# A fused scan and expert kernel: the turn loop written out, the expert tiles moved two units later, the scan output held twice

## What is computed

```python
xn = _layernorm(x)
# branch 1: scan over tokens sorted by cluster (16 states for each of 256 features)
buckets = argmax(scores);  xs = xn sorted by bucket (stable)
x_dbl = einsum('bdl,cd->bcl', u, x_proj_weight)      # dts, Bm, Cm (Cm += prompt)
delta = softplus(einsum('brl,dr->bdl', dts, dt_projs_weight) + bias)
h = exp(d_t * A) * h + (d_t * u_t) * b_t             # step over the tokens
y = einsum('bdn,bn->bd', h, c_t) + D * u             # then back in the order of x
# branch 2: top 2 of 8 experts, weighted by the softmax of their logits
h = silu(xt @ w1[e]) * (xt @ w3[e]);  y = h @ w2[e]
out = x + branch1(xn) + branch2(xn)
```

## Time and profile before

| | |
|---|---|
| median of 3 runs | 818.77 us (815.6 to 820.09) |
| the profiled execution | 817.38 us |
| its span, first to last instruction | 815.3 us |
| DVE busy | 682.9 us (84%) |
| PE busy | 663.9 us (81%) |
| POOL busy | 597.3 us (73%) |
| ACT busy | 431.0 us (53%) |

### The profile page before, as it was taken

How to read it: one execution, slowest core, us unless ns; L and a number is a source line. 1 busy time by engine, 2 the same in 40 slices (tenths; PEclk the granted TensorE clock), 3 DMA queues, 4 the chain that set the end, 5 groups by cost and what they waited for, 6 DMA issues and landing times. The chain is left out here.

```text
span 815.3 us, 15751 instructions
## 1 busy us (share of the span) xinstructions
PE 663.9 (81%) x4538; PEld 422.7 (52%) x4539; DVE 682.9 (84%) x882; ACT 431.0 (53%) x926; POOL 597.3 (73%) x372
## 2 busy tenths in 40 slices
PE   3734889788998798989998898999889798989870
PEld 2523745245655465556655565565556555655550
DVE  5769777579999999999999999999999999997110
ACT  1324656465655556656655575566557554653320
POOL 3728800038788898988989898888989898889532
PEclk9866955599999989999999998999999998999995
DMA  7972659979944754674575466547645654662322
GB/s 228 371 259 91 180 206 297 321 221 241 210 102 103 144 118 87 146 150 94 115 163 111 89 149 138 105 90 164 139 90 125 134 127 90 142 142 35 49 27 26
DMA packets 76845, 118.63 MB, mean 146 GB/s; under 512 B 22456, under 2 KB 56848, under 8 KB 74512
## 3 DMA queue, kind: packets, MB, share of 16 engines
q1 hardware_dynamic: 54656, 90.95, 41.2%
q0 software_dynamic: 19824, 27.16, 19.4%
q10 hardware_dynamic: 2336, 0.15, 0.2%
HBM read 82.87 MB, written 35.27 MB: 145 GB/s over the span
## 5 line engine op out<-in xcount | busy, mean ns | idle before, releaser
L534 POOL TENSOR_TENSOR ring<-ring,bc 128x1024 f32<-128x1024 f32 (+2 forms) x128 | 308.0, 2424 | 38.9 <-DVE state L1047 38.0
L1044 DVE TENSOR_TENSOR_SCAN ring<-ring,state,pb 128x512 f32<-128x512 f32 x256 | 313.8, 1267 | 4.6
L654 ACT ACTIVATE ring<-late,aneg 128x512 f32<-128x512 f32 x256 | 164.2, 721 | 12.0 <-DMA late<-dd_d 9.1
L1035 DVE TENSOR_TENSOR pb<-fb,bc 128x1024 f32<-128x1024 f32 x128 | 157.3, 1229 | 3.0
L1284 PE MATMUL py<-w2x,pool 128*128 x568 | 141.6, 395 | 0.5 <-ACT pool L726 0.3
L1267 PE MATMUL fa<-w,pool 128*128 x284 | 137.7, 608 | 3.9 <-issue 2.8
L506 POOL DMA_INDIRECT out_dram<-pool,meta x71 | 112.9, 1590 | 29.8 <-issue 15.7
L1267 PE MATMUL fb<-w,pool 128*128 x284 | 134.3, 596 | 0.0
L486 POOL DMA_INDIRECT pool<-xn_d,meta x71 | 71.3, 1004 | 81.3 <-DVE ids L1001 33.5
L1284 PEld LDWEIGHTS py<-w2x,pool 128*128 128x128 f32 x568 | 107.7, 200 | 13.6 <-issue 1.0
L1267 PEld LDWEIGHTS fb<-w,pool 128*128 128x128 f32 x284 | 54.5, 192 | 68.9 <-issue 68.9
(11 more groups left out here) (213 smaller groups left out, 752.8 us busy)
## 6 DMA issues: line engine op xcount, KB each, us to landing
late<-dd_d SPq DMA_DIRECT2D x256, 128.0 KB
bc<-bc_d SPq DMA_DIRECT2D x72, 256.0 KB
w<-in_L_ffn_w_dram SPq DMA_DIRECT2D x16, 512.0 KB, 8.6
ring<-in_L_attn_x_dram SPq DMA_DIRECT2D x8, 512.0 KB, 4.3
out_dram<-ring SPq DMA_DIRECT2D x8, 512.0 KB, 7.7
xn_d<-w2x SPq DMA_DIRECT2D x8, 512.0 KB, 8.6
dd_d<-pool SPq DMA_DIRECT2D x8, 512.0 KB
dd_d<-ring SPq DMA_DIRECT2D x8, 512.0 KB, 5.1
```

Of the source, the lines that this page charges most:

```text
L534: ins = po.tensor_tensor(r, r, c_rows, ALU.mult)
L654: ins = ac.activation(ring[:, g % RING, n, :], dd[:, g % 2, 0, :], ACT.Exp, scale=aneg[:, NH * g + n:NH * g + n + 1])
L1035: ve.tensor_tensor(pb[:, :].rearrange("p (n c) -> p n c", n=2), pd[:, :].rearrange("p (o c) -> p o c", o=1).to_broadcast([P, 2, CH]), b_ro ...
L1044: ve.tensor_tensor_scan(r, r, pb[:, CH * m:CH * m + CH], state[:, NH * g + n:NH * g + n + 1], ALU.mult, ALU.add).then_inc(S["scan_done"], 1)
```

## The change

The turn loops of all engines are written out: no registers for addresses, no `apart`, no loop ends.

The tiles move by two turns against the units: in turn u, DVE does the SiLU of tile u - 1 (none in turn 0), then unit u. ACT starts with the exponentials of unit 0, which wait for the preparation's last DVE product (`pr_du`) and no longer for `dd_d`; those of unit 1 wait for parts of it, those of unit 2 for the rest. PE may turn tile 0 once `pr_ab` and `pr_re` are done. Eight tiles (63 to 70) are left behind the last unit in place of six.

`ya` and `yb` become two buffers `ya[c % 2]`; `hand_over` is gone, the scan adds read `ya` and `ids`. `xr` grows from 4 to 6 buffers, `ye` from 2 to 3. The rows of the slot table come in blocks of 8 tiles, one DMA a chunk in place of 8, into 16 slots. The block for the next chunk is loaded in unit 3 of a chunk; it takes the slots of the tiles before, so SP first waits until their last add has landed. SP's wait for PE in each turn goes away.

Of the last unit's products with the C rows, DVE does the second half. The last chunk's four scan adds go after tile 65, side by side. The bank `pd` is no longer used to turn x.

The core of the diff:

```diff
 (SP)
-            def turn(c):
-                for s in range(SPI):
-                    if not (isinstance(c, int) and s < 2):
-                        load_dd(c, s)
...
-                    sp.wait_ge(S["xtr_done"], j + 1)
...
-                    load_meta(j + 3, (s + 4) % SPI, s % 2)
+            for u in range(UNITS):
+                c, g = u // G, u % G
+                if u >= 2:
+                    load_dd(u)
+                if c == 0 and g + EARLY < E:
+                    load_up(g + EARLY, w3, w3_in)
+                    load_down(g + EARLY)
+                if g == 3 and c + 1 < NCH:
+                    if c:
+                        sp.wait_ge(S["hc_done"], G * c)
+                    sp.wait_ge(S["bc_in"], 128 * (c + 1))
+                if 3 <= g < 3 + P // DG and c + 1 < NCH:
+                    load_bc(c + 1, g - 3)
+                if g == 3 and c:
+                    sp.wait_ge(S["meta_in"], 16 * (c + 1))
+                    sp.wait_ge(S["added"], landed_expert(BLOCK * c - 1))
+                    load_meta(c + 1)
 (POOL)
+            for u in range(UNITS):
+                c, g = u // G, u % G
+                j = u - 2
+                if j >= 0:
+                    gather(j + XR)
+                scans = SCAN_UNITS.get(g, ()) if c else ()
+                split = 1 if scans else NH // 2
+                po.wait_ge(S["h_ready"], u + 1)
+                done = multiply(u, slice(0, split))
+                for n in scans:
+                    add_scan(c - 1, n, landed_scan(c - 1, scans[0]) - 16)
+                if u < UNITS - 1:
+                    done = multiply(u, slice(split, NH))
+                elif split < NH // 2:
+                    done = multiply(u, slice(split, NH // 2))
+                done.then_inc(S["hc_done"], 1)
+                if j >= 0:
+                    add_expert(j)
+            for j in range(UNITS - 2, FT):
+                if j + XR < FT:
+                    gather(j + XR)
+                add_expert(j)
+                if j == LAST_SCANS:
+                    for n in range(TPC):
+                        add_scan(NCH - 1, n, landed_expert(j))
 (ACT)
+            def exps(u):
+                ac.wait_ge(dd_in[u % 2], 64 * (u // 2 + 1))
+                if u == 0:
+                    ac.wait_ge(S["pr_du"], KC * NCH)
+                elif u == 1:
+                    ac.wait_ge(S["bc_put1"], 32 * NCH // 2)
+                    ac.wait_ge(S["dd_put10"], 16 * NCH // 2)
+                elif u == 2:
+                    ac.wait_ge(S["dd_put11"], 16 * NCH // 2)
...
+            exps(0)
+            put_du(0)
+            evac_xt(0)
+            exps(1)
+            for u in range(1, FT + 1):
+                j = u - 1
+                tanh(j)
+                if u < UNITS:
+                    put_du(u)
+                if j:
                     evac_ht(j - 1)
+                if 3 <= u < UNITS + 3:
+                    take_y(u - 3)
+                if 2 <= u < UNITS + 2:
+                    take_sum(u - 2)
                 if j + 1 < FT:
+                    evac_xt(j + 1)
+                if u + 1 < UNITS:
+                    exps(u + 1)
+                if j:
+                    evac_y(j - 1)
 (DVE)
+            for u in range(UNITS):
+                if u:
+                    silu(u - 1)
+                half_unit(u, 0)
+                half_unit(u, 1)
+                keep_states(u)
...
+            ve.tensor_tensor(r, r, bc[:, last_u // G % 2, 1, NH // 2:NH, :].rearrange("p n c -> p (n c)"),
+                             ALU.mult).then_inc(S["hc_last"], 1)
+            for j in range(UNITS - 1, FT):
+                silu(j)
```

More of the change, by code:

```diff
@@ L33 @@
 RING = 4
[L34 to L38, removed]
+UNITS = NCH * G
+SCAN_UNITS = {3: (0, 1), 7: (2, 3)}
+XR, XT, YE = 6, 4, 3
+BLOCK = G
 CONST_LOADS, CONST2_LOADS = 5, 8
@@ L243, in apart, with experts_by, scans_by, unit_of_expert @@
             eng.sem_inc(S["passed"], 1)
[L245 to L265, removed]
+        def experts_by(u):
+            return max(0, u - 1)
+        LAST_SCANS = UNITS + 1
+        def scans_by(u):
+            c, g = u // G, u % G
+            return 0 if c == 0 else (c - 1) * TPC + sum(len(SCAN_UNITS[k]) for k in SCAN_UNITS if k <= g)
+        def unit_of_expert(j):
+            return min(j + 2, UNITS - 1)
+        def landed_expert(j):
+            return 16 * (1 + j + 1 + scans_by(unit_of_expert(j)) + (TPC if j > LAST_SCANS else 0))
+        def landed_scan(c, n):
+            u = (c + 1) * G + next(k for k in SCAN_UNITS if n in SCAN_UNITS[k])
+            return 16 * (1 + experts_by(u - 1) + c * TPC + n + 1)
         @block.sync
@@ L509, in add_scan @@
-            def add_scan(turn, c, n, beside=0):
-                po.wait_ge(S["yb_done"], c + 1)
-                if not isinstance(c, int):
-                    apart(po)
-                po.wait_ge(S["added"], landed(turn - 1 - beside))
-                apart(po)
-                po.indirect_dma_start(out[:, :], bass.IndirectOffsetOnAxis(ap=idb[:, n:n + 1], axis=0), yb[:, n, :], None,
-                                      compute_op=ALU.add).then_inc(S["added"], 16)
-            po.wait_ge(S["acc_put"], 16 * NCH)
@@ L541, in _ @@
-            turn(0)
-            with po.Fori(1, NCH) as c:
-                turn(c)
-            for i, (kind, n) in enumerate(REST_ADDS):
-                if kind == "expert":
-                    if n + 4 < FT:
-                        gather(n + 4, (n + 4) % SPI)
-                    add_expert(REST_TURN + i, n, n % SPI, n % 2)
-                else:
-                    add_scan(REST_TURN + i, NCH - 1, n)
-            po.wait_ge(S["added"], landed(REST_TURN + len(REST_ADDS) - 1))
+            for j in range(2, XR):
+                gather(j)
@@ L794, in _ @@
             evac_ht(FT - 1)
[L795 removed]
+            evac_y(FT - 1)
         @block.vector
```

463 lines of the change are left out of this document (159 added, 304 removed).

## The result

The changed kernel takes 831.77 us (median of 4 runs, 829.14 to 835.67), the kernel before 818.21 on the same chips (4 runs, 815.6 to 820.09): a ratio of 1.0172, 95% interval 1.012 to 1.0224. The change makes the kernel slower by 1.7%. The forecast was 810.5. The profiled execution took 830.56, and its span is 828.8, against 815.3 before.

A forecast was written before the change was run, and what follows sets the result against it. DVE's work was taken to bound the turns, POOL's adds the tail. Unit 63's reduction at 738.9 plus a 69.5 us tail gave a span of 808.4; with 2.1 outside it, 810.5 us (range 801 to 817).

The forecast's parts named there:

- Start: Before unit 1: unit 0 runs while `dd_d` lands, winning one whole turn less 0.25 us (-0.6 to +1.3).
- Unit 2: Ahead of unit 2: DVE waits about 2.0 us (0 to 3), its `dd` load being behind two experts' weights.
- Turns written out: Units 1 to 63: 62 turns at 8.893 us, 551.4 us in all, with loop losses and tanh waits gone.
- rival C: All turns: straight code costs instruction fetches, half a us in each of 14 places; 817.5 us; chance 0.07.
- rival A: Chunks: SP's new wait is covered, as `dd` lands within 5.5 us; 803.9 us; chance 0.20.
- The wait that is added: Unit 3 of chunks: SP's wait delays `dd` for unit 8c + 4; DVE waits 6.6 us in all (0 to 11).
- The threshold: Before unit 8c + 4: exponentials may start at latest 5.5 us behind the reduction of unit 8c + 2.
- POOL's lateness in turn 8c + 1: On POOL: the tile add of that turn starts 6.6 us behind that unit's reduction.
- the load itself: Load of `dd` for unit 8c + 4: 3.1 us to bring bytes, perhaps 1.3 more until the semaphore counts.
- Rival B: Chunks: `dd` load takes 6.8 us from issue, queues being shared; DVE waits 3.1 longer in six chunks; 829; chance 0.08.
- rival D: Behind the start or in the tail: tile stream bounds, through PE's lower clock or `ye`; 815.5 us; chance 0.09.
- The tail: Unit 63's reduction to the end: POOL's adds still last, shared products and side-by-side scan adds offset two more tiles; 69.5 us.

## Why the prediction was wrong

The forecast was 21.3 us too low. In the reduction of unit 63, forecast 738.9 and measured 759.62, there are 20.7 of it; -0.3 in the tail, 0.9 outside the span.

**Start: 0.9 too low.** The reduction of unit 1 came at 179.46; my terms put it at 178.6. The exponentials of unit 1 began at 165.29, where I had 165.3, but they didn't set the time. Unit 0 did: I had DVE begin it at 159.5 and be idle behind it, and it began at 163.06 and went over into tile 0's SiLU and unit 1 without a gap. Of these 3.6 us, 1.4 are the preparation, which ended later (its last DVE product at 157.11, before 155.68); in about 2.2 more ACT waited for the load of `dd` for unit 0, which my terms don't have. The idle time that I had forecast took up all but 0.9 us of it. ACT at the start of the changed kernel:

```profile
159.99 2.56 ACT L619 ACTIVATE ring<-late,aneg 128x512 f32<-128x512 f32 x4 [4.44 <-DMA late<-dd_d]
...
165.29 2.56 ACT L619 ACTIVATE ring<-late,aneg 128x512 f32<-128x512 f32 x4 [1.96 <-DMA dd_d<-ring]
167.87 1.28 ACT L679 ACT_TABLE_LOAD   x1
169.16 0.60 ACT L679 ACTIVATE pool<-fa 128x512 f32<-128x512 f32 x1
```

**Unit 2: right.** 2.4 us (the wait itself is 2.26), forecast 2.0.

**Turns written out: right in kind.** 8.89 a turn, no loop ends, so rival C falls. The instruction queues of the page grew from 15 and 14 fetches to 39 and 27, and no turn got longer. The Trainium skill (Runtime: NRT & Kernel Launch, section Instruction fetch mechanics) says that straight code is fetched ahead, mostly hidden, and that a taken branch out of the window is not; the run with only the loops written out agrees, as its seven pieces of about half a us at the loop ends vanished. The rest of my 8 us, the waits for the tanh, didn't all go: with 24 slots, 3.8 of the 6.9 remain beside unit 2 and the clearing. That is most of the distance from rival A's 803.9 to its 808.64. My reason for these waits was wrong too: I took them for a matter of the `ye` buffers, but 3.4 of the 3.8 us follow turns at a granted clock of 0.62. In the kernel before it is the same: its waits ahead of units 14, 38 and 58 (0.6, 1.3 and 0.6 us of loss) follow the three turns at 0.65, 0.62 and 0.62, and such waits came with three buffers as well.

**The wait that is added: the step that failed,** in two ways.

Its direct part was mis-sized, 11.8 us for 6.6. The threshold held to a tenth: in chunks 2 to 7 the exponentials start 6.3, 7.4, 7.9, 7.4, 8.3 and 7.6 us behind the reduction of unit 8c + 2, and the units 8c + 4 lose 0.8, 1.9, 2.4, 1.9, 2.7 and 2.0, which is the one less 5.5. On average it is 7.5 where I had 6.6. Two terms were off. The first is POOL's lateness in turn 8c + 1. I took 6.6 us from a kernel in which no landing held POOL up; in the changed kernel the add is issued 6.5, 9.7, 8.5, 9.7, 7.8 and 8.8 us behind the reduction, since in turn 8c - 1 of the chunks 3 to 7 POOL had already waited for a landing. With 24 slots, where the cause is gone, it is 6.5 in each of the chunks 2 to 7. The wait makes worse the very thing that it waits for, and a number read in the kernel before can't show that. In chunk 2, where POOL was no later than that, unit 20 lost 0.8, the other five 2.2 on average.

The second is the load itself. Two more differences hid POOL's lateness in the sum: the `meta` load goes out 3.8 us after the add's issue, where I had 4.55, and in chunks 3, 5 and 7 DVE had itself lost time ahead of unit 8c + 2 (2.1, 3.5 and 1.1 us), so that the reduction I count from was later as well. By this the load of `dd` goes out 2.8 us behind that reduction on average, about my 2.7. But the exponentials begin 4.2 to 5.7 us after its issue, 4.7 on average, where I had 3.1 to 4.4 and took 3.9.

Its second part, the bunching, was missing whole. Beside 0.3 for the clearing, 14.3 us are lost at units for which I had a cost of nothing. 12.8 of them, at six units, come where a late product meets a turn at lower granted clock; with products in time, such turns cost 3.4 us in all (24 slots). I asked who is queued behind SP's wait and priced the first of them, the `dd` of unit 8c + 4. I didn't ask what the rest of the queue does when it is let go at once, nor what then shares the DMA engines with it. "SP's wait for PE in each turn cost nothing to lose" is part of the same step: without it there is nothing that spreads the backlog, and putting it back gave 14 us.

Rival B named the right cause (others share the queues), but mostly at the wrong place: the load of `dd` took 0.8 us longer than I had taken, not 3.1, and the larger part came through the adds and POOL's queue. It had 0.08, and that its 829 is near the result is luck. The lower clock of PE stands in rival D, for the start and the tail; it showed in the turns.

**The tail: right.** 69.2 us for 69.5. The tiles' adds are 4.4 to 4.7 apart, the scan adds 1.87, the last add 59.9 us behind unit 63's reduction, forecast 60.8 (807.7 - 746.9); from it to the end it is 9.3 where I had 8.7, which makes up for most of that. Side by side alone saves 7.2. The tile stream as the bound of the tail, rival D, isn't seen.

The sum had one term with a margin, and the range around it (0 to 11 us) took in the uncertainty of a load's landing, not a second effect of the same wait. The other parts as they turned out (the turns, the start, the tail) add up to the 808.64 that the kernel takes with 24 slots: 9.6 us of gain that one wait turned into 13.6 of loss.

What stays open: what makes the landing late, the shared DMA engines or something else that it depends on. The runs only show that it comes and goes with the loads beside it. A kernel with the new wait but smaller loads wasn't tried. Open too is whether late products bring PE's lower clock about: it also comes with products in time, in three turns at 0.62 with 24 slots.

## What to carry to other kernels

A wait put into a queue that issues the loads of many consumers has two prices: the first load behind it comes late, and all behind that come together; read the first against the margin of its consumer, the second against whatever small transfer of the critical path will lie among them (here an add of 128 KB). Before a wait that "costs nothing" is taken away, see whether it spaces something out. Where the wait depends on an engine that it can itself make late, a lateness read in the kernel before is a lower end and not an estimate; here eight more slots of the table removed the dependence.

## What the runs showed of the hardware

An indirect DMA that adds 128 KB, and the next instruction that waits for its landing: with little beside it, SP's load left 3.8 us after the add's issue (636.21 to 640.01), and the next add on POOL 4.4 to 4.7 us after it (the tail; 4.55 on average in the earlier trace rows). With 2 MB of loads under way, at a DMA share of 1.04 and 223 GB/s, the next add left 8.8 us after it.

PE's matmuls, the same work at two granted clocks: the fold of a unit took 1.08 us at full clock and 1.94 in the turn at 0.65, the eight products with w2 1.89 and 3.30. With products in time, a turn at 0.62 cost DVE 1.1 to 1.2 us and one at 0.81 nothing in the run with 24 slots; in the run with the loads of the start moved, 1.3 and up to 1.0.

POOL's product of 128x512 took 1.27 us in the run that leaves all to POOL (1.27 in unit 19 too), and 2.31 while DVE made a product of two operands that both lie in SBUF (1.23 us, started 0.05 before it): POOL's ends 1.1 us behind DVE's, about as if it had begun only then. DVE's usual products, whose first operand is in PSUM, and its scans show no such effect on POOL (a product of 128x1024 beside them takes 2.3 us, less than two of 1.27). The Trainium skill (SBUF — State Buffer, section SBUF: two separate sides) says that the two engines share a port pair as an exclusive lock, which a DVE operation with two inputs in SBUF takes for its whole length; the trace agrees, with these numbers. The second product's 1.87 us is no slowing: its record begins at 742.63, while that of the scan add before it on POOL runs to 743.20, and from there it is 1.30. So to give DVE half of POOL's work gained no more than 1.1 us in the tail (69.7 against 70.8).
